# DLRM tower: the first quarter in two units of one tile, with six parts of each unit's bilinear work laid with the batch on the partitions

## What is computed

```python
e = jnp.stack([tbl_0[ids[:, 0]], ..., tbl_31[ids[:, 31]]], axis=1)
idx_i, idx_j = np.triu_indices(F, k=1)
left = jnp.einsum('bpd,pde->bpe', x[:, idx_i, :], W)
z = jnp.sum(left * x[:, idx_j, :], axis=-1)
h = jnp.concatenate([z, dense_ctx], axis=1)
h = jnp.maximum(h @ W_top1 + b_top1, 0.0)
h = jnp.maximum(h @ W_top2 + b_top2, 0.0)
y = h @ W_top3
```

## Time and profile before

| | |
|---|---|
| median of three runs | 724.18 us |
| the profiled execution, its own time | 729.45 us |
| its span | 727.7 us |
| busy: PE / ACT / DVE / POOL | 418.7 / 351.9 / 327.3 / 292.2 us |
| works done (DVE multiplications) | 248 |
| indirect DMAs on POOL | 260 |

### The profile page before, as it was taken

One profiled execution on the slowest core, in us unless ns is written; L12 is line 12 of the kernel. 1 busy time (PEld: TensorE's weight loads), 2 busy tenths in 40 slices (PEclk: granted clock), 3 DMA queues, 4 the chain that ended last, 5 costly groups with the idle time before them and its releaser, 6 DMA issues.

```text
span 727.7 us, 8998 instructions
## 1 busy us (share of the span) xinstructions
PE 418.7 (58%) x2440; PEld 217.8 (30%) x2440; DVE 327.3 (45%) x285; ACT 351.9 (48%) x2639; POOL 292.2 (40%) x350
## 2 busy tenths in 40 slices
PE   0400040003599894312199999433209999999988
PEld 0200020000245551000056555210005555455545
DVE  0000000000399891100099998300017998987771
ACT  0000011002599995100378997410008898998852
POOL 6777777772000007777300000777720000565330
PEclk9955555556599998555599999855558999999999
DMA  9996311110000001111000000111100000000000
GB/s 143 174 169 97 77 26 27 27 25 9 1 1 2 1 1 26 25 28 25 13 1 2 2 1 1 25 26 26 27 11 3 1 1 1 3 2 2 1 1 1
DMA packets 44681, 18.88 MB, mean 26 GB/s; under 512 B 39764, under 2 KB 40280, under 8 KB 44632
## 3 DMA queue, kind: packets, MB, share of 16 engines
q1 hardware_dynamic: 36120, 8.86, 9.2%
q0 software_dynamic: 8512, 9.45, 7.0%
HBM read 18.29 MB, written 0.00 MB: 25 GB/s over the span
## 4 chain that ended last, share of the span: by engine, by line
PE 38%; another core or an unknown queue 34%; issue 14%; ACT 10%; DVE 2%; POOL 0%; POOLq 0%; DVEq 0%; ACTq 0%
PE left L798 12%; PE left L793 11%; ACT row_products L690 9%; PE z_sum L819 6%; PE turned L837 3%; PE turned L859 2%; PE turned L758 1%; PE left L806 1%; PE left L837 1%; DVE row_products L645 1%; ACT X L673 1%; DVE column_products L637 1%; POOL row_products L595 0%; PE left L859 0%
## 5 line engine op out<-in xcount | busy, mean ns | idle before, releaser
L578 POOL DMA_INDIRECT rows<-in_tbl_dram,ids_sb x256 | 242.3, 947 | 285.4 <-DVE row_products L645 206.2
L690 ACT ACTIVATE row_products<-row_products 128x64 f32<-128x64 f32 x1280 | 306.8, 247 | 58.2 <-issue 53.4
L690 ACT ACTIVATION_READ_ACCUMULATOR row_products<-row_products 128x1 f32 x1280 | 248.2, 194 | 42.0 <-issue 42.0
L637 DVE TENSOR_TENSOR column_products<-left,X 128x1024 f32<-128x1024 f32 x104 | 124.2, 1217 | 210.8 <-remote 130.1
L798 PE MATMUL left<-w_sb,X 64*128 64x512 f32 x480 | 131.8, 641 | 119.0 <-issue 118.5
L645 DVE TENSOR_TENSOR row_products<-left,rows 128x1024 f32<-128x1024 f32 x120 | 143.2, 1218 | 101.0 <-remote 68.1
L793 PE MATMUL left<-X,w_sb 64*128 64x256 f32 x960 | 137.1, 417 | 72.3 <-issue 35.3
L793 PEld LDWEIGHTS left<-X,w_sb 64*128 64x128 f32 x960 | 97.0, 203 | 128.2 <-issue 62.0
L673 ACT ACTIVATE X<-turned 128x512 f32<-128x512 f32 (+1 forms) x34 | 19.2, 565 | 210.1 <-remote 173.6
L819 PE MATMUL z_sum<-column_products,ones_window 128*32 128x512 f32 x512 | 79.6, 642 | 33.4 <-issue 23.3
L595 POOL TENSOR_TENSOR row_products<-row_products 128x512 f32<-128x512 f32 (+4 forms) x70 | 42.5, 607 | 123.9 <-DVE row_products L645 119.5
(11 more groups left out here) (30 smaller groups left out, 87.7 us busy)
## 6 DMA issues: line engine op xcount, KB each, us to landing
rows<-in_tbl_dram,ids_sb POOLq DMA_INDIRECT x256
w_sb<-in_W_top_dram SPq DMA_DIRECT2D x1, 512.0 KB
w_sb<-in_L_rec_W_dram SPq DMA_DIRECT2D x1, 496.0 KB
w_sb<-in_L_rec_W_dram SPq DMA_DIRECT2D x1, 480.0 KB
w_sb<-in_L_rec_W_dram SPq DMA_DIRECT2D x1, 464.0 KB
w_sb<-in_L_rec_W_dram SPq DMA_DIRECT2D x1, 448.0 KB
w_sb<-in_L_rec_W_dram SPq DMA_DIRECT2D x1, 432.0 KB
w_sb<-in_L_rec_W_dram SPq DMA_DIRECT2D x1, 416.0 KB
```

What stands on the lines that cost most here:

```text
L578: pool.indirect_dma_start(out=rows[:, q % 2 * QT + t, f * D:(f + 1) * D], out_offset=None, in_=tables[f], in_offset=bass.IndirectOffsetOnA ...
L637: nc.vector.tensor_tensor(to, of, X[:, n:n + 2, :].rearrange("p g b -> p (g b)").unsqueeze(1).to_broadcast([P, 2, BANK]), ALU.mult).then_i ...
L690: ins = nc.scalar.activation(product, product, ACT.Copy, accum_out=z_nat[:, tile, column:column + 1])
```

## The change

The batch is now cut into five units: tile 0, tile 1, then quarters 1, 2 and 3 as before. `rows` is gathered unit by unit; POOL issues the same 260 indirect DMAs, with couple 15 of tile 0 needing two of them rather than four. The gathers of quarter 2 wait for all works of units 0 and 1, those of quarter 3 for all of quarter 1, as before.

What was one part (what a columns work holds) is half as wide in a unit of one tile, so that such a columns work holds two parts: eight calls of 128 columns rather than four of 256, four sums of 256 columns rather than two of 512, and one to four DVE instructions. The two own works of a quarter become one of each unit with 16 calls of 128 columns. In each of the two units six parts are taken out of the columns works and made with the batch on the partitions, as three "parts" works: four calls with 256 moving columns, one multiplication with `rows`, and row sums into a new buffer `z_part`, which POOL clears at the start. When a unit's sums are done, `add` puts `z_part` onto `z_sum` with eight calls against the identity. The works are 248 as before: for quarter 0 now 24 columns, 2 own, 6 parts and 30 rows instead of 30, 2, 0 and 30.

The planner's constants are changed too, a turn is four columns works (eight sums in a wide unit, 16 in a narrow one), and the transposes of weights (`wT`) are now placed by it. In the whole plan ACT has 75 row sums instead of 80, DVE 37 instead of 26, POOL 14 in both.

```diff
+UNITS = [(0, 1), (1, 1), (2, 2), (4, 2), (6, 2)]
+LAST = QUARTERS - 1
...
-TURN = 8
+
+TURN = 4
...
-BATCHES = [2, 2, 2, 1, 1, 1, 1, 2, 2, 2]
+BATCHES = {0: [1, 1, 1, 1, 1, 1, 1, 1, 2, 2, 2, 2], 1: [2, 2, 2, 2, 2, 2, 4]}
...
-WORK, OWN, SUM, SET, TRANSPOSE, LAYER, SWITCH, RELOAD = 0.87, 1.85, 0.215, 0.15, 0.12, 1.72, 0.1, 0.12
-MULTIPLY, ROWSUM_DVE, ROWSUM_ACT, ROWSUM_POOL, COPY, RELU, SIGNAL = 1.23, 1.23, 3.9, 4.8, 0.6, 0.47, 0.12
-GATHER, LANDING, W_FIRST, W_PAIR = 5.0, 9.5, 6.0, 0.1
-ACT_SLACK, DVE_SLACK, MARGIN, NEAR, LAST_LEAD, POOL_AFTER = 1.5, 0.6, 1.0, 0.3, 0.15, 4.0
+MLP_APART = 4
+X_WAIT, MLP_WAIT, LATER = 10, 24, 2
+
+
+WORK, NARROW, OWN, SUM, SET, TRANSPOSE, LAYER, ADD, SWITCH, RELOAD = 0.85, 1.2, 1.85, 0.215, 0.15, 0.12, 1.72, 0.6, 0.1, 0.12
+MULTIPLY, ROWSUM_DVE, ROWSUM_PARTS, ROWSUM_ACT, ROWSUM_POOL, COPY, RELU, SIGNAL = 1.23, 1.23, 1.6, 3.8, 4.8, 0.6, 0.47, 0.12
+GATHER, LANDING, W_FIRST, W_PAIR = 2.5, 9.5, 6.0, 0.1
+ACT_SLACK, DVE_SLACK, MARGIN, NEAR, LAST_LEAD, POOL_AFTER = 1, 0.8, 0.3, 0.3, 0.6, 4.0
...
+ROW_PAIRS = [(3, 4), (9, 10), (11, 12), (14, 15), (17, 18), (20, 21), (22, 23), (24, 25), (29, 30)]
+PAIRS = ROW_PAIRS + [(0, 1), (2, 5), (7, 8), (13, 16), (19, 26), (28, 31)]
+
+ON_PARTITIONS = [ROW_PAIRS[:3], ROW_PAIRS[:3], [], [], []]
...
     columns, rows = [], []
-    for q in range(QUARTERS):
-        single = None
+    for u, (first, tiles) in enumerate(UNITS):
+        turned = [a for x in ON_PARTITIONS[u] for a in x]
+        if tiles == QT:
+            columns += [("own" if a in OWN_PARTS else "columns", u, (a,)) for a in range(len(PARTS)) if a not in turned]
+        else:
+            columns += [("columns", u, x) for x in sorted(PAIRS) if x not in ON_PARTITIONS[u]] + [("own", u, tuple(OWN_PARTS))]
+        pieces = [("parts", u, first + t, x) for x in ON_PARTITIONS[u] for t in range(tiles)]
         for m in range(FP - 1, -1, -1):
-            ks = column_groups(m)
-            if m % 8 == 0:
-                columns.append(("own", q, m))
-            if len(ks) % 2:
-                if single is None:
-                    single = (m, ks[-1])
-                else:
-                    columns.append(("columns", q, (single, (m, ks[-1]))))
-                    single = None
-                ks = ks[:-1]
-            columns += [("columns", q, ((m, k), (m, k + 1))) for k in reversed(ks[::2])]
-            rows += [("rows", q, QT * q + t, m, c) for c in row_chunks(m) for t in range(QT)]
+            pieces += [("rows", u, first + t, m, c) for c in row_chunks(m) for t in range(tiles)]
+        rows += sorted(pieces, key=lambda x: -least_field(x))
...
+            nc.gpsimd.memset(z_part[:, :, :, :], 0.0).then_inc(part_zeroed, 1)
             pool.wait_ge(ids_loaded, 16)
-            for q in range(QUARTERS):
-                if q >= 2:
-
-                    pool.wait_ge(multiplied, work_of_quarter[q - 2])
-                if q == 1:
+            for u, (first, tiles) in enumerate(UNITS):
+                if before(u) is not None:
+
+                    pool.wait_ge(multiplied, work_until[before(u)])
+                if u == 2:
...
                             pool.indirect_dma_start(
-                                out=rows[:, q % 2 * QT + t, f * D:(f + 1) * D], out_offset=None, in_=tables[f],
-                                in_offset=bass.IndirectOffsetOnAxis(ap=ids_sb[:, QT * q + t, f:f + 1], axis=0),
-                            ).then_inc(rows_gathered[q % 2][m], 16)
+                                out=rows[:, t % (2 * QT), f * D:(f + 1) * D], out_offset=None, in_=tables[f],
+                                in_offset=bass.IndirectOffsetOnAxis(ap=ids_sb[:, t, f:f + 1], axis=0),
+                            ).then_inc(rows_gathered[u][m], 16)
...
+                else:
+                    z_part_free(dve, x[1])
+                    for p, a in enumerate(in_row(x)):
+                        for o in (0, 1):
+                            row = part_column(a, o, 0, 0)
+                            ins = nc.vector.tensor_reduce(
+                                z_part[:, x[2] % QT, :, row:row + 2],
+                                products[:, o, QB * p:QB * (p + 1)].rearrange("p (g j d) -> p g j d", g=2, d=D), AX.X, ALU.add)
...
+                if x[0] == "parts":
+                    t = x[2] % QT
+                    for p, a in enumerate(in_row(x)):
+                        (m, k), (m2, k2) = PARTS[a]
+
+                        for g, (m, k, n) in enumerate([(m, k, 2)] if m == m2 else [(m, k, 1), (m2, k2, 1)]):
+                            column = QB * p + 2 * D * g
+                            for odd in (0, 1):
+                                ins = nc.tensor.matmul(left[:, s, odd, column:column + 2 * D * n],
+                                                       X[D * odd:D * odd + D, base + m, P * t:P * (t + 1)],
+                                                       weights(odd, m, k, 2 * n), start=True, stop=True)
+                    ins.then_inc(projected, 1)
+                    return
+                for p, part in enumerate(PARTS[a] for a in x[2]):
+                    at = 2 * span * p
+                    if x[0] == "columns":
+                        for g, (m, k) in enumerate(part):
+                            for odd in (0, 1):
+                                ins = nc.tensor.matmul(left[:, s, odd, at + span * g:at + span * (g + 1)], weights(odd, m, k, 2),
+                                                       X[D * odd:D * odd + D, base + m, of_batch], start=True, stop=True)
...
+                for w, p, o, v in sums[begin:sums_until[n]]:
+                    same = [b for b in sums_of_unit[u] if b % 4 == v % 4]
+                    r, t = v % 4, v // 4
+                    nc.tensor.matmul(z_sum[32 * r:32 * r + 32, 0:2 * span], ones_window[:, 30 - 2 * t:62 - 2 * t],
+                                     column_products[:, n % COLUMN_PRODS, o, 2 * span * p:2 * span * (p + 1)],
+                                     start=(v == same[0]), stop=(v == same[-1] and not ON_PARTITIONS[u])).then_inc(summed, 1)
...
+            def add(u):
+
+                first, tiles = UNITS[u]
+                wait_row_sums(pe, 1 + max(n for n, w in enumerate(row_work) if work[w][:2] == ("parts", u)))
+                for t in range(tiles):
+                    for g in (0, 1):
+                        column = width(u) * g + P * t
+                        for r in range(4):
+                            ins = nc.tensor.matmul(z_sum[32 * r:32 * r + 32, column:column + P],
+                                                   z_part[:, (first + t) % QT, g, 32 * r:32 * r + 32], ident[:, :],
+                                                   start=False, stop=(t == tiles - 1 and g == 1))
+                ins.then_inc(added, 1)
```

More of the change, by code:

```diff
@@ new lines, in make_work, with on_partitions, until, width @@
+    return columns, rows
+def on_partitions(x):
+    return x[0] in ("rows", "parts")
+def until(pieces):
+    return [sum(x[1] <= u for x in pieces) for u in range(len(UNITS))]
+def width(u):
+    return P * UNITS[u][1]
+def quarter(u):
+    return UNITS[u][0] // QT
+def last_unit(q):
+    return max(u for u in range(len(UNITS)) if quarter(u) == q)
+def before(u):
+    return last_unit(quarter(u) - 2) if quarter(u) >= 2 else None
+def least_field(x):
+    return min(fields_of(x))
+def fields_of(x):
+    if x[0] == "rows":
+        return [x[3]]
+    fields = set()
+    for part in (PARTS[a] for a in x[-1]):
+        fields |= set(range(part, part + 8)) if isinstance(part, int) else {m for m, k in part}
+    return sorted(fields)
@@ L156, in __init__ @@
         self.columns, self.rows = make_work()
+        self.columns_until, self.rows_until = until(self.columns), until(self.rows)
         self.batches = make_batches()
@@ L164, in __init__ @@
         self.row_end, self.sum_end, self.z_end = {}, {}, {}
-        self.sums = self.batch = 0
+        self.turn_ends = [n + 1 for n in range(len(self.columns)) if n + 1 in self.columns_until
+                          or (n + 1 - max([0] + [e for e in self.columns_until if e <= n])) % TURN == 0]
+        self.turns = self.batch = 0
+        self.turned = []
         self.x_ready = {}
@@ L325, in take_work @@
     def take_work(self, x, begin):
-        length = OWN if x[0] == "own" else WORK
+        narrow = not on_partitions(x) and UNITS[x[1]][1] < QT
+        length = (1.3 * OWN if narrow else OWN) if x[0] == "own" else NARROW if narrow else WORK
         self.on_pe(x[0] == "own", begin, length)
@@ L330, in take_work @@
         begin = max(self.dve, self.pe + SIGNAL)
-        if x[0] == "rows" and n >= ROW_PRODS:
+        if on_partitions(x) and n >= ROW_PRODS:
             begin = max(begin, self.row_end[n - ROW_PRODS])
-        self.dve = begin + (2 if x[0] == "own" else 1) * MULTIPLY
+        self.dve = begin + (2 if x[0] == "own" else 1.1 if narrow or x[0] == "parts" and x[3] not in ROW_PAIRS else 1) * MULTIPLY
         self.work.append(x)
```

(16 more changed lines are left out.)

426 lines of the change are left out of this document (277 added, 149 removed).

## The result

The changed kernel takes 735.9 us (median of four: 731.4, 733.23, 738.58, 740.01), the kernel before 724.09: a ratio of 1.0161, 95% interval 1.0089 to 1.0233. It is slower by 12 us, where 6.5 were forecast (730.7, range 720.5 to 742). The four executions lie 8.6 us apart, so the 12 us are known to some 5 either way. The profile shows the slowest of them, 740.01 us; it took 10.6 us more than the profiled execution of before.

The account below looks back on a forecast made before the run. The prediction saw three gather stages with PE at 2.8 us a pair and PE-bound full-speed stages between. Terms 5.9 + 0 + 0.6 = +6.5 us took 724.2 to 730.7 us, range 720.5 to 742.

Parts of the forecast that it names:

- What bounds the kernel: Whole kernel: three gather stages with PE at 2.8 us a pair whenever POOL gathers, three full-speed stages between and behind.
- Gathers: POOL's indirect DMAs: count stays 260, the first 132 again end near 168 us, nothing gained or lost.
- Head start: First gather stage: first work on PE near 20 us instead of 30.4, 11 works done at 187 instead of 8.
- rival B: First gather stage: slow pace starts near 20 us, costing about four works, 5.8 us; 736.5 us in all; chance 0.18.
- The narrow pair, 0.093 us: PE at full speed, first quarter: a narrow columns work's 16 pairs cost 0.093 us each, 1.49 us a work.
- rival A: PE from 187 us to third gathers: narrow pair 0.056 us, head start wins, DVE sets pace; -3.4, 720.8 us; chance 0.22.
- PE has 8.9 us more: First quarter's remainder at 187 us: PE's work grows from 67.7 to 76.6 us, head start already counted.
- What hides of it: Full-speed stage after 187 us: PE's idle time, about 3 us, absorbs part of 8.9, leaving 5.9.
- If PE were not the fuller engine ... DVE sets the pace: Full-speed stage after 187 us: the remaining 5.9 us would then shrink to nothing.
- Later quarters 0: Later quarters: same works, sums and layers; extra DVE row sums lie beside PE; 0 us, within -3 to +3.
- gather stages +0.6: Two later gather stages: four works again in the second, about one fewer in the third; 0 to 1.5, taken 0.6 us.
- D: The forecast itself: PE-bound, +3 to +12 us, 730.7 us; upper end has a narrow pair at 0.11 us; chance 0.52.

Follow-up runs that it names:

- held copy: Kernel before and changed kernel, PE made to wait for last gathered rows where slow stretches ended, on a chip without slow pace: 697.11 and 707.53 us.
- r13: Changed kernel with PE waiting for gathered rows ahead of works 9, 78 and 134, eight works done first instead of six: 702.18 us.
- r14: New planner, first quarter as one unit, no parts, PE waiting for gathered rows ahead of works 9, 78 and 135: 692.84 us.
- r15: Changed kernel with PE waits for gathered rows, DVE's first-quarter row sums reading 8 of 64 numbers: 735.45 us, 1.0161 of the kernel before.
- r16: Changed kernel with PE waits for gathered rows, five of DVE's first-quarter row sums given to ACT: 750.35 us, 1.0368 of the kernel before.

## Why the prediction was right, and where it was not

*What bounds the kernel*: right for the slow pace of 2.8 us a pair, but not "whenever POOL gathers": the gathers begin at 3.45 and the pace near 31, and on chips 7 to 9 it never comes. "PE is cold there" isn't what the rows show either: from 24 to 36 us the granted clock was 1.00, its upper level (2.4 GHz), in the kernel before. Why PE was slower there the rows don't say.

*Gathers*: right. The first 132 end at 167.20 + 0.94, each later stage takes 80 us.

*Head start, "11 are done at 187 instead of 8"*: wrong, 6. This is the step that failed. I let the slow pace begin at 31 us as before and counted four works ahead of it. It began near 20, in the first work, after about as many pairs as before. That is rival B, which I gave 0.18. B priced four lost works at 5.8 us, 1.45 each. Five were lost, and in the held copy two works cost 5.4, 2.7 each. So B's price was too low, and that its 736.5 is so near 735.9 is luck. B also didn't count that a narrow work has twice the pairs of a wide one and so costs 45 us in that pace.

*The narrow pair, 0.093 us*: wrong, 0.060. A work's price is 0.96, not 1.49: 21 x 0.53 = 11 us too much. This was nearly rival A's number (0.056), and A's reason, that pairs are paced by the moving columns, fits: half the columns take about half of a wide pair's 0.11.

*"PE has 8.9 us more"*: these two errors have opposite signs. By my own prices five works fewer done are 7.3 us more and the cheap pairs 11 less, so 8.9 becomes 5.2. Quarter 2's gathers were predicted to start at 285 to 292 and start at 288.67; that is luck in these two terms, and the rest came from a term that I did not have, below. PE is busy 91.78 us there with 63 works, 79.44 with 58 before: 12.3 us more, of which five works more are 7 (an estimate at 79.44 / 58 each).

*"What hides of it", 3 us of PE's idle time*: wrong. The idle time was not filled but grew: between 200 and 270 us PE was busy 65.36 of 70, so 4.6 idle, where it had been 2.6.

*"If PE were not the fuller engine ... DVE sets the pace"*: half right. DVE became the fuller one. I had seen its 11 extra row sums and put them beside PE in the later quarters, but ten of them (eight of rows works, two of parts works) stand in this stage, where DVE had been busy 74.25 of 86. The term missing from my sum is r13 against r14, +5.5 in the stage and +9.3 in all. In the stage it is 1.6 us of PE's work and 3.9 of PE's idle time, 3.1 of them waits for DVE. r15 gives some 3.2 of the stage to the length of the row sums. How the rest divides between DVE's narrow instructions and the order in which the plan puts its work stays open, and so do the 4 us behind quarter 2's gathers.

*Later quarters 0, gather stages +0.6*: right in the sum. From quarter 2's gathers to the end the changed kernel takes 449.4 us and the one before 454.8; with three works of 1.5 us fewer the accounts differ by 1 us. The count of works was off: the two later gather stages yielded six and nine works before, not four to five each, and eight and eight now.

So the sign and the range held, but by another mechanism: B's early onset of the slow pace and a stage in which DVE is laden and PE waits for it, rather than D's dear pair. That the number held is in good part luck.

## What to carry to other kernels

Work cut into narrower pieces for an earlier start has to be priced on every engine: here PE paid little for half-wide matmuls, but DVE paid 0.68 us for each half where the whole cost 1.22, and where each pair has a fixed price (2.8 us here) narrow work costs double. A full engine is not yet the bound: cut its work and see whether the stage follows. Price a plan at the pace that the chip will have when it runs. The same change is 1.6% slower where the slow pace is and 0.6% faster on a chip without it. The version that beats both kernels in each comparison in which it ran is the new planner with whole quarters (425.08 against 429.86 and 427.1; held 692.84 against 697.11 and 707.53). It was not run on a chip with the slow pace.

## What the runs showed of the hardware

The same program takes 724 us on chip 0 and, in most executions, 428 to 430 on chips 7, 8 and 9, with POOL's indirect DMAs at 947 ns each in both. On the one kind PE's pairs take 2.8 us over most of the time in which they are issued, on the other they keep their pace. What makes the kinds differ no run here shows, nor that it is the chip alone: of 22 executions of the kernel before on chip 7 one took 573.12 us (granted clock 0.674) and one 2143.47 (1.0), and of five on chip 9 one took 1302.28, all without a trace. The chip of the first measurements isn't recorded, but its 724.09 us are chip 0's 724.46, and the three slow stretches of the changed kernel are in r15 and r16 too.

On chip 0's kind the slow pace first began after 13 to 15 pairs in each of four profiles: by the first product 28.4 us behind the first work in the changed kernel, about nine slow pairs in r15 and r16 (first works at 19.00 and 19.31, products at 44.88 and 44.14), and 5.5 faster pairs of the first work in the kernel before. But a time fits as well as a count: PE's first transposes stand at 18.63 before, 8.04 in the changed kernel, 7.81 in r15 and 8.06 in r16, and the pace came 12 to 13 us after them in all four, an estimate. No run tells the two apart, and neither explains the second and third stretch.

The Trainium skill, page "SBUF — State Buffer", section "Who interferes with whom", says that PE and ACT never wait on anyone. On chips 7 to 9 the traces agree: PE keeps its pace beside POOL's gathers. On chip 0 its pairs take 2.8 us; what they wait for no trace shows, so it stays open whether that is the kind of waiting the page speaks of.
